# Pass end, first feed-forward chunk and T products of a graph/feed-forward kernel rebuilt: three edge-sum buffers, finishing in six blocks, spread semaphore clears, matrix lows in quarters

## The reference

```
x = x + gnn0(_layernorm(x))        # graph attention, 4 heads, over 21250 edges
x = x + ffn0(_layernorm(x))        # 4 experts, thresholded gates
x = x + gnn1(_layernorm(x), edge_attr)   # mean of the edge attributes by node, then two matmuls
x = x + ffn1(_layernorm(x))        # 8-head self-attention, then mixture of 8 experts
# gnn0:
q, k, v = (x @ W + b).reshape(n, H, OUT_DIM)
alpha = einsum('ehc,ehc->eh', q[dst], k[src]) / sqrt(OUT_DIM)
attn = softmax of alpha over the edges of one dst
agg = segment_sum(attn[:, :, None] * v[src], dst)
x_attn = agg + x @ Wskip + bskip
h = x_attn @ Wlin + blin + x_attn[:, :OUT_DIM]
return gamma * (h - mean) / sqrt(var + 1e-05) + beta
# ffn0:
hidden = relu(einsum('ni,ehi->neh', xf, fc1_w))
out = weights * (hidden @ lora_A @ lora_B @ fc2_w)
```

## Time and profile before

| what | us, where nothing else stands |
|---|---|
| median of 3 runs | 1955.11 (1953.63 to 1959.61) |
| the profiled execution, its own time | 1956.35 |
| span of the profile | 1954.7 |
| PE busy | 1777.9 (91%) |
| DVE busy | 1314.1 (67%) |
| ACT busy | 907.0 (46%) |
| POOL busy | 590.2 (30%) |
| PE's mean granted clock over the span | 0.96 of full speed |

### The profile page before, as it was taken

How to read it: one execution, slowest core, us unless ns; L and a number is a source line. 1 busy time by engine, 2 the same in 40 slices (tenths; PEclk the granted TensorE clock), 3 DMA queues, 4 the chain that set the end, 5 groups by cost and what they waited for, 6 DMA issues and landing times. The chain is left out here.

```text
span 1954.7 us, 31926 instructions
## 1 busy us (share of the span) xinstructions
PE 1777.9 (91%) x10958; PEld 1544.2 (79%) x10958; DVE 1314.1 (67%) x2945; ACT 907.0 (46%) x1652; POOL 590.2 (30%) x531
## 2 busy tenths in 40 slices
PE   7998969899999999898679999999899999999496
PEld 5776769888888888676567998988688888888385
DVE  5444336688888888378664565645578787886676
ACT  4332236677777776222131234324365555555421
POOL 0000030365555652111100021122254545444244
PEclk9999989999999999899889999999999999999698
DMA  6652495677777775656233027976010211113432
GB/s 239 210 187 86 144 302 194 188 207 203 202 201 203 200 204 141 157 142 153 72 106 92 1 84 151 198 207 210 19 33 17 58 31 32 31 32 120 160 120 87
DMA packets 183532, 265.14 MB, mean 136 GB/s; under 512 B 55852, under 2 KB 102443, under 8 KB 181109
## 3 DMA queue, kind: packets, MB, share of 16 engines
q1 hardware_dynamic: 117839, 169.58, 29.9%
q0 software_dynamic: 49920, 62.94, 12.1%
q10 hardware_dynamic: 15640, 30.90, 6.5%
HBM read 198.55 MB, written 85.86 MB: 145 GB/s over the span
## 5 line engine op out<-in xcount | busy, mean ns | idle before, releaser
L1063 POOL DMA_INDIRECT edge_rows<-xn_store,edge_index x200 | 245.2, 1226 | 254.1 <-PE psum L138 104.3
L2539 POOL TENSOR_TENSOR mprob<-mprob,mrden 125x1250 f32<-125x1250 f32 x80 | 181.7, 2273 | 218.4 <-DVE mrden L2645 218.0
L2568 ACT ACTIVATE mprob<-psum,mbias 125x1250 f32<-125x1250 f32 x80 | 104.4, 1305 | 153.4 <-DVE mbias L2654 153.4
L1279 DVE TENSOR_TENSOR edge_xt_lo<-psum,edge_xt_hi 128x500 fp32r<-128x500 f32 x200 | 134.8, 675 | 52.6 <-ACT edge_xt_hi L1156 52.6
L2652 DVE TENSOR_REDUCE mmin<-psum 125x1 f32<-125x512 f32 (+1 forms) x240 | 126.8, 583 | 47.7 <-PE psum L2811 47.5
L1156 ACT ACTIVATE edge_xt_hi<-psum 128x500 fp32r<-128x500 f32 x200 | 117.8, 590 | 87.8 <-PE psum L1442 87.8
L2829 PE MATMUL psum<-ident,mprob 125*125 125x125 f32 x800 | 117.9, 292 | 18.6 <-DVE ptm_lo L2659 9.4
L2829 PEld LDWEIGHTS psum<-ident,mprob 125*125 125x125 f32 x800 | 100.3, 191 | 36.2 <-DVE ptm_lo L2659 20.2
L2659 DVE TENSOR_TENSOR ptm_lo<-psum,ptm_hi 125x500 fp32r<-125x500 f32 (+1 forms) x240 | 126.3, 581 | 2.0 <-ACT ptm_hi L2574 2.0
L1442 PE MATMUL psum<-ident,edge_rows 125*128 125x125 f32 x800 | 120.0, 273 | 3.7 <-DVE edge_xt_lo L1279 2.0
L1308 DVE TENSOR_TENSOR edge_rows_lo<-edge_rows,edge_rows_hi 125x1024 fp32r<-125x1024 f32 x100 | 121.1, 1211 | 0.0
(11 more groups left out here) (519 smaller groups left out, 5370.4 us busy)
## 6 DMA issues: line engine op xcount, KB each, us to landing
slots_in<-blank_rows ACTq DMA_DIRECT2D x20, 1026.0 KB, 16.2
t_store<-t_part SPq DMA_DIRECT2D x20, 1000.0 KB, 5.3
t_row<-t_store SPq DMA_DIRECT2D x47, 400.0 KB, 6.8
y_store<-y_rows SPq DMA_DIRECT2D x50, 200.0 KB
q_chunk<-q_store SPq DMA_DIRECT2D x40, 250.0 KB, 5.4
y_tile<-y_store SPq DMA_DIRECT2D x10, 896.0 KB
edge_attr<-in_attr SPq DMA_DIRECT2D x50, 112.0 KB
moe_xg<-slots_in SPq DMA_DIRECT2D x17, 256.5 KB, 3.5
```

The source lines that it names most:

```text
L1063: nc.gpsimd.indirect_dma_start(xe[t % RING][:, s, :], None, g.xn_store, bass.IndirectOffsetOnAxis(ap=index[t % RING][:, s, 0:1], axis=0)). ...
L1279: nc.vector.tensor_tensor(xt_lo[:, k, :], x_bank(KT * t + k), f32(xt_hi[:, k, :]), ALU.subtract).then_inc(x_low, 1)
L2539: nc.gpsimd.tensor_tensor(prob[:, n % 4, :], prob[:, n % 4, :], rden[:, n % 4:n % 4 + 1].broadcast_to([P, N]), ALU.mult).then_inc(p_ready, 1)
```

## The change

The T products get a third `part` buffer; SP loads one `v_raw` in each head, at chunk 1, in place of three in the first, and issues the 20 `consts` DMAs in four groups of five, at chunks 2 and 4 of heads 1 and 2. The skip product turns over five banks. POOL gathers two windows before the T products are stored, and windows 2, 3 and 4 each behind the last store of one `part` buffer; `landed(2)` stands behind `gather(4)`. In the pass end `hot` and `attr_hl` have three buffers and are made two turns ahead; finishing has six steps (10 to 15), with `fin.result` at step 13; the first fc1 matrix is split there by quarters, top and low, at turns 34 to 37; part of the semaphores is cleared at window 3 of SP's list and the rest while the last store is under way; the next pass's ranges are computed ahead of the last tile. In chunk 0 of the feed-forward layer fc1 is split by quarters after each unit, finishing of tiles 8 and 9 is spread over experts 0 to 2, and their turns, the gates and the edge means come later. Of w2 the second half is split behind units 4 to 7.

```
+    PARTS_HELD = 3
+    part = [at(f"t_part{i}", [128, NC_W, WIN, 2 * KT], F32R, 28 + 8 * i) for i in range(PARTS_HELD)]
...
-    hot = [at(f"edge_hot{i}", [P, SLOTS_E, P], F32R, 76 + 2 * i) for i in range(2)]
+    HOTS = 3
+    hot = [at(f"edge_hot{i}", [P, SLOTS_E, P], F32R, kb) for i, kb in enumerate((76, 78, 66))]
...
+    attr_hl = [at(f"edge_attr_hl{i}", [P, SLOTS_E, ATTR], F32R, kb) for i, kb in enumerate((52, 54.0625, 63))]
...
-        return core.bank(3 + t % 3)[0:P, :]
+        return core.bank(3 + t % SKIP_BANKS)[0:P, :]
...
+                    if c == 1:
+                        if h == 1:
                             sp.wait_ge(pool_made, EDGE_ROW)
-                        sp.dma_start(v_raw[c][:], g.vl_store[c]).then_inc(v_in, 16)
+                        sp.dma_start(v_raw[h][:], g.vl_store[h]).then_inc(v_in, 16)
+                    if h in (1, 2) and c in (2, 4):
+                        head = 2 * (h - 1) + c // 2 - 1
+                        for pos in range(PER_TILE):
+                            sp.dma_start(consts[WIN * head:WIN * head + WIN, NT * pos:NT * pos + NT],
+                                         g.cd[WIN * pos:WIN * pos + WIN, NT * head:NT * head + NT]).then_inc(fin_in, 16)
                     sp.wait_ge(u_low, KT * i + KT)
                     sp.dma_start(g.t_store[NC_W * c:NC_W * (c + 1), :, h, :].rearrange("w p x -> p w x"),
-                                 f32(part[i % 2][:]).rearrange("p w n q -> p w (n q)")).then_inc(part_stored[i % 2], 16)
+                                 f32(part[i % PARTS_HELD][:]).rearrange("p w n q -> p w (n q)")).then_inc(part_stored[i % PARTS_HELD], 16)
                 if h + 2 < HEADS:
                     m_in(h + 2)
             skip_over(sp)
...
+                    if t == 3:
+                        for s in edge_inner:
+                            sp.sem_clear(s)
...
-                sp.wait_ge(base_out, 32 * NC)
                 sp.sem_inc(pass_over, 1)
                 for s in inner:
                     sp.sem_clear(s)
+                sp.wait_ge(base_out, 32 * NC)
+                sp.sem_clear(base_out)
...
+            pool.wait_ge(fin_in, 32)
+            nc.gpsimd.tensor_tensor(fin.row0[:], fin.row0[:], row0b[:], ALU.add).then_inc(pool_made, 1)
             pool.wait_ge(fin_in, ROWS_IN)
-            nc.gpsimd.tensor_tensor(fin.row0[:], fin.row0[:], row0b[:], ALU.add).then_inc(pool_made, 1)
             nc.gpsimd.tensor_scalar(bound[:], consts[:], scale, -scale * NO_EDGE, ALU.mult, ALU.add).then_inc(pool_made, 1)
...
-                if t >= 2:
-                    pool.wait_ge(agg_done, t - 1)
-                    nc.gpsimd.memset(f32(hot[t % 2][:, :, window(t - 2)]), 0.0).then_inc(hot_clear, 1)
+                if t >= HOTS:
+                    pool.wait_ge(agg_done, t - HOTS + 1)
+                    nc.gpsimd.memset(f32(hot[t % HOTS][:, :, window(t - HOTS)]), 0.0).then_inc(hot_clear, 1)
...
-                gather(2)
-                for t in range(3):
+                for t in range(2):
                     landed(t, turn)
-                parts_over(pool)
-                gather(3)
-                gather(4)
+                for t, i in ((2, 2), (3, 0), (4, 1)):
+                    part_over(pool, i)
+                    gather(t)
+                landed(2, turn)
                 landed(3, turn)
                 for t in range(1, WINDOWS):
...
-                                act.wait_ge(v_first if h == 0 else v_in, 16 if h == 0 else 16 * (HEADS - 1))
+                                act.wait_ge(v_in, 16 * h + 16)
...
-                attr_hi(0)
+                attr_hi(0), attr_hi(1)
                 for n in range(TURNS):
                     if n + 2 < TURNS:
                         yt_tops(n + 2)
-                    for t in sums_behind(n + 1):
+                    for t in sums_behind(n + 2):
                         attr_hi(t)
-                act.wait_ge(g.fc1_in, 16 * turn + 16)
-                nc.scalar.activation(g.fc1_hi0[:], g.fc1_raw0[:], ACT.Copy).then_inc(g.fc1_top, 1)
-                act.wait_ge(g.fc1_top, turn + 1)
+                    k = n - FC1_TURN
+                    if 0 <= k < KT:
+                        if k == 0:
+                            act.wait_ge(g.fc1_in, 16 * turn + 16)
+                        nc.scalar.activation(g.fc1_hi0[:, k, :], g.fc1_raw0[:, k, :], ACT.Copy).then_inc(g.fc1_top, 1)
                 act.sem_inc(pass_done, 1)
...
+            def fc1_first(turn, k):
+                dve.wait_ge(g.fc1_top, KT * turn + k + 1)
+                link(nc.vector.tensor_tensor(g.fc1_lo0[:, k, :], g.fc1_raw0[:, k, :], f32(g.fc1_hi0[:, k, :]), ALU.subtract))
...
+                    fin.spread(nc, link, c, g.acc)
                 if step == 11:
+                    fin.first_root(nc, link)
+                if step == 12:
+                    fin.second_root(nc, link)
+                if step == 13:
                     fin.centred(nc, link, c)
                     dve.wait_ge(xin_ready, c + 1)
                     for s in range(2):
                         fin.result(nc, c, s, g.acc).then_inc(xin_used, 1)
-                if step == 13:
+                if step == 14:
                     dve.wait_ge(xin_used, 2 * c + 2)
-                    fin.moments(nc, link, c, g.acc)
+                    fin.spread(nc, link, c, g.acc)
+                    fin.moments(nc, link, c)
+                if step == 15:
+                    fin.scale(nc, link, c)
 
             passes = dve.value_load(g.passes_i[0:1, 0:1], min_val=1, max_val=2 * ROUNDS - 1)
             dve.wait_ge(pool_made, TABLES)
...
-                hots(0)
-                attr_lo(0)
+                for t in range(2):
+                    hots(t)
...
-                    for t in sums_behind(n + 1):
+                    for t in sums_behind(n + 2):
                         hots(t)
                         attr_lo(t)
+                    if 0 <= n - FC1_TURN < KT:
...
+                nc.vector.tensor_copy(bound[:], nb[:])
+                link(nc.vector.tensor_scalar(g.turn_f[:], g.turn_f[:], 1.0, None, ALU.add))
+                link(g.pass_ranges(nc, link))
                 add_out(NT - 1)
                 edge_sums(NT - 1)
-                nc.vector.tensor_copy(bound[:], nb[:])
-                link(nc.vector.tensor_scalar(g.turn_f[:], g.turn_f[:], 1.0, None, ALU.add))
-                g.pass_values(nc, link).then_inc(pass_done, 1)
+                g.pass_flags(nc).then_inc(pass_done, 1)
                 dve.wait_ge(pass_go, turn + 1)
-            link = core.link.on(dve)
-            link(nc.vector.tensor_scalar(rcount[:], count[:], 1.0, None, ALU.max))
-            link(nc.vector.reciprocal(rcount[:], rcount[:]))
-            nc.vector.tensor_tensor(g.agg[:], g.agg[:], rcount[:].unsqueeze(2).broadcast_to([P, NT, EDGE_D]), ALU.mult)
 
         @block.tensor
...
+    fc1_hi = [g.fc1_hi0] + [at(f"fc1_hi{i + 1}", [128, KT, D], F32R, kb) for i, kb in enumerate((108, 116, 124))]
+    fc1_lo = [g.fc1_lo0] + [at(f"fc1_lo{i + 1}", [128, KT, D], F32R, kb) for i, kb in enumerate((132, 140, 148))]
...
-                            copy_x(4 + m)
-                        if c == 0 and e == 2:
                             if m == 0:
                                 act.wait_ge(all_xs, 8)
                                 act.wait_ge(x_copied, 8)
-                            top(fc1_hi[3], fc1_raw[3], fc1_in[3], fc1_h[3], m)
+                            top(fc1_hi[2], fc1_raw[2], fc1_in[2], fc1_h[2], m)
+                        if c == 0 and e == 2 and m:
+                            if m == 1:
+                                act.wait_ge(fin_done, 2)
+                            top(fc1_hi[3], fc1_raw[3], fc1_in[3], fc1_h[3], m - 1)
                         if c and e == 3 and m < 2:
                             rows_hi(2 * (c - 1) + m, row_bank(m))
                         if c == LAST - 1 and m == 3:
...
+                    if c == 0 and e == 2:
+                        top(fc1_hi[3], fc1_raw[3], fc1_in[3], fc1_h[3], KT - 1)
+                        for t in range(8, NT):
+                            first_hi(t)
+                    if c == 0 and e == 3:
+                        edge_tops()
+                        gate_exponentials()
...
+                    if c == 0 and m >= MT - KT:
+                        top(w2_hi[1], w2_raw[1], w2_in[1], w2_h, m - MT + KT)
...
+            last_pair = NC - 1
...
+                            if m < 2:
+                                fc1_bottom(1, 2 * m), fc1_bottom(1, 2 * m + 1)
...
+                            fc1_bottom(2, m)
                             if m == 0:
-                                fin.centred(nc, link, NC - 1)
+                                fin.spread(nc, link, last_pair, g.acc)
+                            if m == 1:
+                                fin.first_root(nc, link)
+                            if m == 2:
+                                fin.second_root(nc, link)
```

(48 more changed lines are left out.)

169 lines of the change are left out of this document (81 added, 88 removed).

## The result

The changed kernel takes 1934.38 us (median, 1930.34 to 1936.75) against 1957.36 for the kernel before in the same session: ratio 0.9882, interval 0.9856 to 0.9908. The forecast was 1931. The kernel before is 2.2 us slower here than in the runs that the forecast started from (1955.11), so the ratio says 1932 on the forecast's own scale. The profiled execution took 1933.92 us against 1956.35, so 22.4 us are to be found in the trace; the sum of the prediction had 25.8.

The account below looks back on a forecast made before the run. PE was taken to bound the kernel, so each stage is worth PE's gaps. Terms 2.9 + 22.0 - 9.2 + 1.2 + 1.9 + 4.0 + 3.0 = 25.8 us gave 1931 us, own range 1921 to 1941, eight-in-ten range 1908 to 1944.

Parts of the forecast that it names:

- Skip and T products: Five banks end PE's first skip wait, 2.9 us; later tables and a third buffer remove T-product gaps, 22.0 us.
- Rival B: DMAs of the T products bind, so their 22.0 us gain shrinks to 12; 1940 us, chance 0.15.
- Start of the loop: Window loop's start: POOL enters late behind the tables, PE waits 7.3 us for window 2; a loss of 9.2 us.
- `landed(2)` stands behind twelve gather issues whatever lands: Loop's start: POOL signals window 2 only after gathers 2, 3 and 4, 18.1 us at the least, at 359.6.
- Pass end: DVE's long-block waits go, but PE waits 3.4 us three times for window attributes; a net gain of 1.2 us.
- the chain as drawn: Pass end: results, fin_x landing, POOL's addition, clear of hot, attributes, moments, then PE's low at 10.3 us.
- the 7.5 us: Pass end: PE's longest wait, for window 4's attributes, was to stay, since SP's list ahead is unchanged.
- Exit: End of the pass: clears (3.2) and edge means (1.3) hidden, last addition 2.6 later; gain 1.9 us.
- First chunk: First feed-forward chunk: early low and waits go, ACT's wait for fc1[3] costs PE 2.3 us; gain 4.0 us.
- Next layer: w2's second half split behind units 4 to 7 shrinks PE's wait of 3.9 us; gain 3.0 us.
- Rival A: Lists work as ordered: loop's start costs only 4 us, pass end gains 11; 1915 us, chance 0.22.
- Rival C: Tables land only with the T products' end, POOL enters the loop late; 10 us slower, 1966 us, chance 0.05.

Follow-up runs that it names:

- tables_only: The kernel before with only the 20 table loads moved from ahead of the first store of T products into heads 1 and 2; ratio 0.9921.
- ffn_late: The changed kernel with ACT's four tops of the fourth fc1 matrix moved behind expert 2 and the tops of tiles 8 and 9; ratio 0.9862.
- tables_early: The changed kernel with the 20 table loads issued in heads 0 and 1 instead of 1 and 2; ratio 0.9882.
- hots2_xin: xin_late with two edge-sum buffers instead of three and windows made ready one turn later; ratio 0.9765.
- best2: The changed kernel with xin_late, ffn_late, tables_early, an earlier third gather, window 4's attributes and the last tile's addition earlier, POOL's first feed-forward clears held; ratio 0.9716.
- xin_late: The changed kernel with SP's load of the next pair's x and POOL's addition to it four windows later; ratio 0.9781.
- pool_late: The changed kernel with only POOL's addition to fin_x four windows later, SP's load left in place; ratio 0.9885.

## Why the prediction was right in sum, step by step

**Skip and T products: right.** 24.9 forecast, 26.3 found: 22.0 and 21.9 for the T products, 2.9 and 4.4 for the skip product. The first store goes out at 228.9 (forecast near 232), and PE has no wait of more than 0.1 us named up to 334. `tables_only` shows the split that the prediction left open. Rival B is out: no part was late with three buffers.

**Start of the loop: right place, sized too high in this profile.** 9.2 forecast, 4.0 found; 3.2 to 8.4 over eight profiles. The failing step is "`landed(2)` stands behind twelve gather issues whatever lands". Its signal reached PE before POOL had begun the third of these gathers, in this profile and in the seven others with that list, so the list does not hold it. What was left to wait for is the landing of gather 2, 5.9 us behind the start of its last issue here and 7.9 in `ffn_late`, where PE waits 4.0. The landing of gathers 0 and 1 was slower than taken (POOL stands 9.4 us instead of 5.7), and PE had a wait of 2.4 us for rows of T that I didn't have. By the Trainium skill (DMA: Bandwidth & Descriptors, Anatomy of one DMA) a load costs some 2.0 us fixed; the trace disagrees again, with 5.3 us for the index loads and 4.7 in `tables_early`.

**Pass end: right mechanism, wrong sign.** +1.2 forecast, -3.8 found. The three waits are there, with the chain as drawn and the 7.5 us unchanged (6.9). My low came where forecast: PE's turn starts 10.8 us behind the results at 828.3 (10.3 forecast). At the first pair PE was due 4.8 us behind them and not 6.9, and waits 6.0; there that estimate is the mis-sized term. At the two others it was due 6.6 us behind them and the low came at 10.8 and 11.0, so it waits 4.2 and 4.4 where 3.4 were forecast. In all, PE waits as long as before (6.9 + 14.6 + 1.0 against 22.7); what is new is the clock, 0.83 in three stretches of 20 us where before it was 0.91 once and 1.00 otherwise. I charged lost clock at the loop's start and forgot it here: four waits of 3.8 in two pieces each became three longer ones. Whether it matters that "ACT and DVE now want" the attributes "one turn earlier" stays open: `hots2_xin` undid that only where SP's wait was out of the way.

**Exit: wrong.** +1.9 forecast, -3.3 found (from PE's last edge sum to the next block). DVE's last instruction comes 7.9 us behind PE's last edge sum, before it was 2.6: the fourth pair's results and moments now follow the last window instead of holding it, and this isn't the 2.6 that I counted but 5.3. And of the 50 clears only 20 moved away; 29 wait for DVE's end as before. With the edge means it makes 2.0 us, not 4.5.

**First chunk: wrong.** 4.0 forecast, 1.4 found. Of the 2.2 us ahead of the first rows 1.1 came: the first of DVE's rows takes 2.04 us beside POOL's clear of 1.80. With that clear held back (`best2`) the four rows take 1.92 us together and not 3.97. The Trainium skill (SBUF — State Buffer, "SBUF: two separate sides") calls the port pair that DVE and GpSimd share an exclusive lock for a whole instruction; the trace agrees: the two instructions start at 957.4 and end at 959.5 and 959.2. Inside, PE's waits for hidden lows fell by 5.1 us (not counted), the wait for a low of fc1 stayed at 2.3 of 3.2, and ACT's wait for fc1[3] cost PE 7.2 us and a clock of 0.73 from 990 to 1015, not 2.3: behind ACT stands DVE's finishing, and behind that the rows of tile 8.

**Next layer: small.** 3.0 forecast, 1.9 found; PE's wait for the low fell from 3.9 to 2.4 (under 2 was forecast). The time of that stage varies from profile to profile by more than the 1.9, with the same code, so only the shorter wait can be put down to the change.

Sum: 26.3 - 4.0 - 3.8 - 3.3 + 1.4 + 1.9 = 18.5, and 4.0 in untouched stages (by rounding of marks 3.9). The forecast held partly by luck: the loop's start was sized 5.2 too high, pass end, exit, chunk and next layer 5.0, 5.2, 2.6 and 1.1 too favourably, and 4.0 came from stages with the same code, which no term covers. Rival A's premise for the pass end, lists that are in time, is what `xin_late` made true: the 11 us that it gave the pass end were 18 against the kernel before (158.3 against 176.7). The 4 us that it gave the loop's start are what was found, though with other waits than it had. Rival C was refuted: the tables landed at 308.

What stays open: why the next layer's first product, whose code is the same in the changed kernel and in the nine made from it, takes 118 to 125 us from first matmul to last in their profiles (PE waits there for ACT, 4.4 us in `best2` and 0.4 in the changed kernel), which is more than most of the experiments gained, and why rows of T land later than before.

## What to carry to other kernels

When a result is moved back in one engine's list, look for the queue that waits for it and move that queue's wait as well: here a load four windows later in SP's list, with POOL's addition that hangs on it, was worth 20 us, nearly as much as the whole change. Ask too what the moved work will now run beside: POOL's addition moved alone gained nothing, where it fell beside DVE's small instructions. Charge each concentrated wait of PE with the clock behind it, some 1.5 us for each us waited here in all (22.2 us for 14.6). And undo a new buffer by itself: the third edge-sum buffer bought nothing once SP's load was moved, and the third part buffer 2 us, while the order of 20 small loads bought 20 in its stage and 15.5 of the kernel's time.

## What the hardware showed that was not expected

A wait in POOL's list is passed while gathers ahead of it are still to be issued: `landed(2)` stands behind twelve issues of 1.5 us that began at 344.3, and its signal is raised at 354.8, with five of them not begun. The profile's times of POOL are rough, but the order is the same in all eight profiles with that list. A tiny instruction of DVE can last until POOL's beside it is over: 2.33 us for a 125 x 2 operation (median 0.16) at 935.23, beside an addition of POOL from 935.12 of 2.41, and 1.77 us in place of 0.17 in `pool_late`.
